# Attention and top-2 experts on one core: a last attention unit with an order of its own, a tanh router, and the low weight halves on GpSimd

## The chip, the core and the metric

One core of one Trainium2 chip. The time is the device time of one execution in microseconds (us), the median of the runs. The profile shows one execution; its span runs from the first to the last instruction.

## The reference

x is 32 sequences of 128 tokens of 128 features, and ctx has the same shape. Two layers follow each other, each with a residual:

```python
x = x + attention(layernorm(x), ctx, ctx)          # 16 heads of 8, linear attention, causal
# q' = elu(q) + 1, k' = elu(k) + 1; out_t = q'_t . sum_{s<=t} k'_s v_s^T; divided by cumsum(q')
x = x + experts(layernorm(x))
# conf = sigmoid(x conf_w^T + conf_b); bids = conf * wealth; the best two of 8 experts are taken
# weights = softmax(the two best bids); expert: (silu(x gate^T) * (x up^T)) down^T, inner size 512
```

## The kernel before

One program writes an order of instructions by hand for each engine, and semaphores tie them together. It has two stages.

**Attention stage.** The 32 sequences are taken in eight units (u = 0 to 7) of four sequences b. `body(u)` of each engine works on unit u and, interleaved with it, on the front of unit u+1 (layer norm, projections, elu) and on the tail of unit u-1 (output projection, second layer norm, router, the places of its tokens among the experts). On TensorE the attention itself is `scores(u, b)` (L1206) and `values(u, b)` (L1223). ScalarE copies the off-diagonal scores (`off_scores`, L693), VectorE masks the diagonal ones (`mask_scores`, L894). VectorE scans Z (`front_z`), and Z's inverse is a seed by an Exp on ScalarE (`z_seed`), `front_zerr` (L884), two Squares (`z_series`) and `front_rz` (L889, L892). `tail_o` (L906) multiplies the values by it, and `tail_out` (L1248 the bias, L1252 the projection) goes to x by `tail_x1` (L911). GpSimd makes the inverse deviation of both layer norms (`front`, `tail`, L481 to L486).

The router of unit u-1 is: logits (L1263, L1266), `tail_exp1` (L714) on ScalarE, add, reciprocal, multiply by wealth on VectorE (L926 to L928), the maxima (L931) and their difference (L933), `tail_exp2` (L720) on ScalarE, and `tail_weights` (L499 to L507) on GpSimd, with a power that takes the inverse. `tail_choose` (L945 to L949), `tail_rank` (TensorE) and `tail_place` (L954 to L964) find the row of each token. GpSimd's `tail_rows` (L513) makes the low halves of the rows and `scatter` (L527) writes them by indirect DMA to the DRAM array by_expert, one unit later; eight scatters a unit.

Each expert's weights (gate, up and down, m = 0 to 2) are loaded to `w_raw` (two buffers) and split in two float16 halves: w_hi on ScalarE (`weights`, L634, three instructions) and w_lo on VectorE (L970, three instructions). Expert u is split in unit u. The load of expert u into its buffer waits, on SP's queue, until the low halves of expert u-2 are made; the loads of the next units stand behind it in that queue.

In unit 7 the same `body` runs without the front of a unit 8; it also has `full_count`, `full_segments` and `full_tiles` (L984 to L998), the table of the first 16 tiles. On GpSimd it sends half of unit 5's rows, then makes unit 6's deviation (`tail(6)`), and then sends the rest of unit 5. The tail of unit 7 and the dispatch of units 6 and 7 lie in the first tiles of the next stage.

**Tile stage.** Rows that chose the same expert are taken in 31 tiles of 256 and then 9 of 128. SP loads a tile's rows with a transposing DMA (L432), the first only when all the rows of units 0 to 5 have been dispatched. TensorE does `gate_up` (L1360 to L1362) of tile i, then `down` (L1380 to L1382) of tile i-1. ScalarE does Silu (L785) and the high half (L792), VectorE the product (L1126) and the low half (L1132); GpSimd writes the result rows to by_token (L616). At the end by_token is read back, added to x and stored. Silu is in another table of ScalarE than Exp: `silu_warm` (L815) stands between the stages, and the router of unit 7 comes back to Exp in tile 4.

Lines of the order that the prediction uses, GpSimd in unit 7 and after it:

```python
if last(u): dispatch(u - 2, [0, 1])
if not first(u): tail(u - 1)
...
dispatch(u - 2, [2, 3]); tail_weights(u - 1, 1 - par)
tail_rows(6); dispatch(6, range(3)); tail(7); dispatch(6, [3])
```

## Time and profile before

| | us |
|---|---|
| median of 3 runs | 402.58 |
| the runs | 405.7, 402.58, 398.73 |
| span of the profiled execution | 364.5 |
| median less span | 38.1 |
| units 1 to 6, from one L906 to the next | 20.0 each |
| unit 7, from its L906 of unit 6 (151.38) to the first gate matmul (177.27) | 25.9 |

The profiled execution's own time is not marked among the runs; the table gives its span. The difference to the median is the time before the first and after the last instruction, to within the spread of the runs (7.0 us). The page's busy shares are: TensorE 81%, VectorE 76%, ScalarE 64%, GpSimd 57% of the span.

### The profile page before, as it was taken

What the parts mean: (1) busy time and instruction counts of PE and PEld (TensorE: products, weight loads), DVE (VectorE), ACT (ScalarE), POOL (GpSimd) and SP (SyncE); (2) the same over time, 40 slices, a digit from 0 to 9 for tenths busy, and PEclk for the clock granted to TensorE, in tenths of its full rate; (3) what the DMA queues carried; (4) which work ended last, traced back from release to release, by engine and by line L of the source; (5) the groups of instructions that cost most, each with busy time, mean ns of one, the idle gap of its engine ahead of it and who ended that gap; (6) DMA issues with size and microseconds to landing.
All of it is one profiled execution on the core that took longest, in us unless ns stands there. A gap on an engine that the chain in (4) does not pass through costs nothing.

```text
span 364.5 us, 12299 instructions
## 1 busy us (share of the span) xinstructions
PE 297.0 (81%) x4430; PEld 246.5 (68%) x4430; DVE 276.2 (76%) x770; ACT 232.9 (64%) x464; POOL 207.5 (57%) x301
## 2 busy tenths in 40 slices
PE   7678897979798888777998899999999799998200
PEld 5456675747475656566687789999988689987100
DVE  5898999999999999993675687976666466564165
ACT  3686969777795959613649786777676476665100
POOL 6301137787868787884686758777554245463300
PEclk9999999999999999755599999999999899999755
DMA  7413120505051310110333314547675796321098
GB/s 239 154 23 125 46 104 10 187 12 190 17 174 34 110 54 21 42 32 31 59 76 74 58 43 104 152 86 170 153 218 154 143 213 161 69 70 28 18 349 325
DMA packets 47722, 39.45 MB, mean 108 GB/s; under 512 B 32550, under 2 KB 39084, under 8 KB 47664
## 3 DMA queue, kind: packets, MB, share of 16 engines
q1 hardware_dynamic: 43344, 30.20, 30.6%
q0 software_dynamic: 4320, 8.47, 8.0%
q8 instruction: 38, 0.62, 0.7%
q14 instruction: 20, 0.16, 0.2%
HBM read 15.16 MB, written 12.21 MB: 75 GB/s over the span
## 4 chain that ended last, share of the span: by engine, by line
PE 29%; DVE 27%; SPq 10%; POOL 10%; issue 9%; DMA 7%; ACT 7%; POOLq 0%; DVEq 0%; ACTq 0%
DVE Pm L899 6%; POOL by_expert L527 5%; SPq L432 3%; PE bank L1360 3%; DMA w_hi<-by_token 3%; PE bank L1380 2%; DVE w_lo L970 2%; PE bank L1362 2%; PE bank L1361 2%; PE scores L1362 2%; PE scores L1361 2%; PE scores L1360 2%; PE bank L1381 2%; PE bank L1382 2%; DVE stats L823 2%
## 5 line engine op out<-in xcount | busy, mean ns | idle before, releaser
L616 POOL DMA_INDIRECT by_token<-y_sb,row_meta x71 | 72.3, 1018 | 61.1 <-ACT y_sb L776 45.3
L1126 DVE SCALAR_TENSOR_TENSOR hid<-scores,silu 128x512 f32<-128x512 f32 x71 | 48.4, 690 | 44.3 <-PE scores L1362 38.6
L527 POOL DMA_INDIRECT by_expert<-token_rows,rows_to x64 | 63.9, 999 | 23.1 <-issue 17.1
L785 ACT ACTIVATE silu<-bank 128x512 f32<-128x512 f32 x71 | 42.0, 596 | 30.0 <-PE bank L1362 29.6
L792 ACT ACTIVATE hid_hi<-hid 128x512 f16<-128x512 f32 x71 | 44.2, 628 | 20.1 <-DVE hid L1126 19.0
L1219 PE MATMUL scores<-qT,Kexp 32*128 32x128 f32 (+1 forms) x1024 | 40.1, 294 | 20.5 <-DVE Pm L899 17.5
L1132 DVE TENSOR_TENSOR Kexp<-hid,hid_hi 128x512 f16<-128x512 f32 x71 | 48.3, 690 | 10.3 <-ACT hid_hi L792 7.5
L1219 PEld LDWEIGHTS scores<-qT,Kexp 32*128 32x128 f32 x1024 | 35.2, 203 | 29.3 <-DVE Pm L899 24.5
L1380 PE MATMUL bank<-w_hi,hid_hi 128*128 x248 | 43.7, 220 | 0.2 <-DVE Kexp L1132 0.2
L1381 PE MATMUL bank<-w_lo,hid_hi 128*128 x248 | 43.6, 220 | 0.0
L1382 PE MATMUL bank<-w_hi,Kexp 128*128 x248 | 43.5, 220 | 0.0
L899 DVE TENSOR_TENSOR Pm<-scores,causal 128x512 f32<-128x512 f32 x64 | 41.1, 684 | 2.3 <-ACT Pm L698 1.8
L1360 PE MATMUL bank<-xgT,w_hi 128*128 128x256 f16 x124 | 34.7, 280 | 6.4 <-DMA xgT<-by_expert 3.6
L698 ACT ACTIVATE Pm<-scores 128x512 f32<-128x512 f32 x32 | 18.8, 586 | 30.5 <-PE scores L1219 30.5
L1361 PE MATMUL bank<-xgT,w_hi 128*128 128x256 f16 x124 | 34.7, 280 | 0.0
L1362 PE MATMUL bank<-xgT,w_lo 128*128 128x256 f16 x124 | 34.7, 280 | 0.0
L1360 PE MATMUL scores<-xgT,w_hi 128*128 128x256 f16 x124 | 34.5, 278 | 0.0
L1361 PE MATMUL scores<-xgT,w_hi 128*128 128x256 f16 x124 | 34.4, 278 | 0.0
L1362 PE MATMUL scores<-xgT,w_lo 128*128 128x256 f16 x124 | 34.4, 278 | 0.0
L1235 PE MATMUL bank<-Pm,Vexp 128*32 128x64 f32 (+1 forms) x1024 | 30.3, 264 | 1.6 <-DVE Pm L899 1.6
L1235 PEld LDWEIGHTS bank<-Pm,Vexp 128*32 128x32 f32 x1024 | 24.5, 117 | 7.4 <-issue 3.3
L1380 PEld LDWEIGHTS bank<-w_hi,hid_hi 128*128 128x128 f16 x248 | 24.5, 99 | 0.7 <-issue 0.4
(291 smaller groups left out, 729.7 us busy)
## 6 DMA issues: line engine op xcount, KB each, us to landing
w_raw<-in_w_pack_dram SPq DMA_DIRECT2D x8, 768.0 KB
x_all<-in_x_tok_dram SPq DMA_DIRECT2D x8, 256.0 KB, 5.6
cT<-in_ctx_t_dram SPq DMA_DIRECT2D x8, 256.0 KB, 5.4
w_hi<-by_token SPq DMA_DIRECT2D x4, 512.0 KB, 7.5
w_lo<-by_token SPq DMA_DIRECT2D x4, 512.0 KB, 8.1
out_dram<-x_all SPq DMA_DIRECT2D x8, 256.0 KB, 6.1
by_expert<-pad_row SPq DMA_DIRECT2D x9, 130.0 KB
by_token<-y_sb,row_meta POOLq DMA_INDIRECT x71
```

The costliest lines, as they stand in the source:

```text
L527: pool.indirect_dma_start(by_expert, bass.IndirectOffsetOnAxis(ap=rows_to[u % 2][:, s, b:b + 1], axis=0), token_rows[u % 2][:, b, s, :], N ...
L616: pool.indirect_dma_start(by_token, bass.IndirectOffsetOnAxis(ap=row_number[:, i % METAS, s, 1:2], axis=0), y_sb[:, k, s, :], None, bounds ...
L899: dve.tensor_tensor(Pm[:, b % 2, :, at:at + CH].rearrange("p (r j) t -> p r j t", r=RG), score_groups[:, :, :, at:at + CH], causal[:].unsq ...
L1126: dve.scalar_tensor_tensor(hid[:, slot, :], bank[2 + slot], 1.0 / WSCALE, silu[:, slot, :], ALU.mult, ALU.mult).then_inc(hid_done, 1)
L1219: ins = pe.matmul(scores4[:, r, j * SPAN + at:j * SPAN + at + n], Kexp[par][rows, c, 2 * j:2 * j + 2, :], qT[par][rows, c * CH:c * CH + n] ...
L1235: ins = pe.matmul(bank[6][32 * r:32 * r + 32, c * CH:c * CH + n], Vexp[par][:, c, 2 * r:2 * r + 2, :].rearrange("p g k -> p (g k)")[:, 16 ...
L1360: pe.matmul(ps, high, x_hi, start=(c == 0), stop=False, skip_group_check=True)
L1361: pe.matmul(ps, high, x_lo, start=False, stop=False, skip_group_check=True)
L1362: ins = pe.matmul(ps, low, x_hi, start=False, stop=True, skip_group_check=True)
L1380: pe.matmul(ps, hid_hi[:, k % 2, slot, h], high, start=(c == 0 and s == 0), stop=False, skip_group_check=True)
L1381: pe.matmul(ps, hid_hi[:, k % 2, slot, h], low, start=False, stop=False, skip_group_check=True)
L1382: ins = pe.matmul(ps, hid_lo[:, k % 2, slot, h], high, start=False, stop=(c == IC - 1), skip_group_check=True)
```

## The change

- Unit 7 gets a `last_body` of its own on TensorE, ScalarE, VectorE and GpSimd. `tail_out(7)` moves from tile 0 to the end of the unit; `tail_rank(6)` and `tail_place(6)` move from the unit to tile 0. The warm-up of Silu moves into the unit, behind the last Exp.
- The router computes sigmoid and the softmax of two by Tanh. VectorE's three instructions L926 to L928 become one. GpSimd's four (L499 to L507) become two small ScalarE instructions that write the weights.
- The high halves of an expert are made one unit ahead (expert 0 before unit 0, expert 1 at the end of unit 0, expert u+1 in unit u from then on). The low halves of experts 0 to 2 are made on GpSimd, with two instructions for each of three parts (a multiplication in place and a subtraction), in units 0 and 1; those of experts 3 to 7 on VectorE in units 2 to 6. SP's waits for a free buffer follow.

```diff
 # GpSimd
+            def low(x, m):
+                pool.wait_ge(whi_done, 3 * x + m + 1)
+                cols = slice(x * (3 * I) + m * I, x * (3 * I) + (m + 1) * I)
+                pool.tensor_scalar(w_raw[x % 2][:, m, :], w_raw[x % 2][:, m, :], WSCALE, None, ALU.mult).then_inc(wx_done, 1)
+                pool.wait_ge(wx_done, 3 * x + m + 1)
+                pool.tensor_tensor(w_lo[:, cols], w_raw[x % 2][:, m, :], w_hi[:, cols], ALU.subtract).then_inc(wlo_pool, 1)
             def body(u, par):
+                front(u + 1)
+                if first(u):
+                    for m in range(3):
+                        low(0, m)
+                    for m in range(2):
+                        low(1, m)
+                if u == 1:
+                    low(1, 2)
                 if u >= 2:
                     tail_rows(u - 2, par)
                 if not first(u):
                     tail(u - 1)
+                if u == 1:
+                    for m in range(3):
+                        low(2, m)
...
+            def last_body(u, par):
+                tail_rows(u - 2, par)
+                dispatch(u - 2, [0, 1])
+                tail(u - 1)
+                dispatch(u - 2, [2, 3])
+                tail_rows(u - 1, 1 - par)
+                tail(u)
+                dispatch(u - 1, [0, 1])
             def tile_step(i, k):
...
+                if i < 2:
+                    dispatch(UNITS - 2, [2 + i])
-                if i == 4:
-                    tail_weights(UNITS - 1, (UNITS - 1) % 2)
 # ScalarE
-                act.activation(conf_e[:], tail_bank(u)[...], ACT.Exp, scale=-1.0).then_inc(lg_exp, 1)
+                act.activation(conf_t[:], tail_bank(u)[...], ACT.Tanh, scale=0.5).then_inc(lg_tanh, 1)
-                act.activation(vexp[:], vdiff[:], ACT.Exp).then_inc(vexp_act, 1)
+                act.activation(vtanh[:], vdiff[:], ACT.Tanh, scale=0.5).then_inc(vtanh_done, 1)
+            def tail_weights(u, par):
+                act.wait_ge(vtanh_done, u + 1)
+                for s, sign in enumerate((-1.0, 1.0)):
+                    act.activation(token_rows[par][:, :, s, D], vtanh[:], ACT.Identity, bias=half_scale[:],
+                                   scale=sign * 0.5 / WSCALE).then_inc(weights_done, 1)
+            def last_body(u, par):
+                off_scores(u, 0)
+                off_scores(u, 1)
+                z_seed(u)
+                off_scores(u, 2)
+                tail_norm(u - 1, 1 - par)
+                act.activation(silu_warm[:], bq_one[:], ACT.Silu)
+                off_scores(u, 3)
+                tail_x2(u - 1, 1 - par)
+                z_series(u)
+                tail_rows(u - 1, 1 - par)
+                tail_tanh1(u - 1)
+                tail_tanh2(u - 1)
+                tail_weights(u - 1, 1 - par)
 # VectorE
-                done(dve.tensor_scalar(conf[:], conf_e[:], 1.0, None, ALU.add))
-                done(dve.reciprocal(conf_e[:], conf[:]))
-                done(dve.tensor_tensor(bids[:], conf_e[:], wealth_b.unsqueeze(1).to_broadcast([P, UB, E]), ALU.mult))
+                dve.scalar_tensor_tensor(bids[:], conf_t[:], 1.0, wealth_half[:].unsqueeze(1).to_broadcast([P, UB, E]),
+                                         ALU.add, ALU.mult).then_inc(router, 1)
+            def last_body(u, par):
+                tail_o(u - 1, 1 - par)
+                full_segments()
+                mask_scores(u, 0)
+                tail_x1(u - 1)
+                tail_stats(u - 1)
+                tail_aggregate(u - 1)
+                mask_scores(u, 1)
+                front_z(u, par)
+                full_tiles()
+                mask_scores(u, 2)
+                front_zerr(u)
+                mask_scores(u, 3)
+                front_rz(u)
+                tail_o(u, par)
+                tail_bids(u - 1)
+                tail_choose(u - 1)
             def tile_step(i, k):
+                if i == 0:
+                    tail_x1(UNITS - 1)
                 hidden(i, k, 0)
+                if i == 0:
+                    tail_place(UNITS - 2)
 # TensorE
+            def last_body(u, par):
+                full_count()
+                tail_out(u - 1)
+                scores(u, par, 1)
+                values(u, par, 0)
+                scores(u, par, 2)
+                values(u, par, 1)
+                scores(u, par, 3)
+                tail_x2(u - 1, 1 - par)
+                values(u, par, 2)
+                tail_logits(u - 1)
+                values(u, par, 3)
+                tail_out(u)
 # TensorE, tile 0
-                        tail_out(UNITS - 1)
+                        tail_rank(UNITS - 2)
 # SP
-                    sp.wait_ge(wlo_done, 3 * (u - 1))
+                if 2 <= u < 2 + POOL_LOWS:
+                    sp.wait_ge(wlo_pool, 3 * (u - 1))
+                elif u >= 2:
+                    sp.wait_ge(wlo_dve, 3 * (u - 1 - POOL_LOWS))
```

## Rows read from the trace of the kernel before

**Rows 1.** The page: TensorE's granted clock in 40 slices of the span.
```profile
PEclk9999999999999999755599999999999899999755
```

**Rows 2.** Busy us of each engine in stretches (stretch, length, engines, clock, DMA share, GB/s).
```profile
111.00:131.00 20.00, 17.00 (x333) 12.61 (x332) 19.42 (x72) 15.69 (x31) 16.23 (x25) 1.00 0.27 75
131.00:151.00 20.00, 14.94 (x293) 10.89 (x291) 19.41 (x72) 15.69 (x31) 16.21 (x25) 0.99 0.09 30
151.00:161.00 10.00, 8.62 (x99) 6.33 (x95) 9.30 (x31) 2.75 (x5) 8.05 (x11) 0.50 0.09 28
161.00:171.00 10.00, 6.55 (x78) 5.73 (x78) 5.01 (x11) 3.45 (x7) 7.26 (x9) 0.50 0.13 42
192.00:202.00 10.00, 8.38 (x87) 7.19 (x85) 5.72 (x9) 8.45 (x18) 6.98 (x8) 1.00 0.31 74
202.00:212.00 10.00, 8.27 (x99) 7.38 (x97) 6.99 (x29) 8.43 (x16) 5.46 (x6) 1.00 0.27 48
212.00:232.00 20.00, 19.97 (x247) 18.52 (x245) 16.61 (x39) 14.65 (x30) 15.69 (x18) 1.00 0.42 102
```

**Rows 3.** Timeline of unit 6: the router on VectorE (start us, us, instruction).
```profile
145.56 0.17 DVE L926 TENSOR_SCALAR conf<-conf_e 128x32 f32<-128x32 f32 x1
...
146.39 0.16 DVE L931 MAX8 top<-bids 128x8 f32<-128x8 f32 x1
```

**Rows 4.** Timeline of unit 0, and GpSimd's wait before unit 1.
```profile
15.93 1.66 ACT L634 ACTIVATE w_hi<-w_raw 128x512 f16<-128x512 f32 x3
...
23.36 1.87 DVE L970 SCALAR_TENSOR_TENSOR w_lo<-w_raw,w_hi 128x512 f16<-128x512 f32 x3
23.41 0.60 ACT L698 ACTIVATE Pm<-scores 128x512 f32<-128x512 f32 x1 [0.86 <-PE scores L1219]
...
33.30 0.20 POOL L481 TENSOR_TENSOR nm<-zero,mv 128x4 f32<-128x4 f32 x1 [19.79 <-DVE mv L827]
```

**Rows 5.** Timeline of unit 1: low halves on VectorE beside ScalarE.
```profile
41.15 1.87 DVE L970 SCALAR_TENSOR_TENSOR w_lo<-w_raw,w_hi 128x512 f16<-128x512 f32 x3
...
42.06 0.58 ACT L698 ACTIVATE Pm<-scores 128x512 f32<-128x512 f32 x1
```

**Rows 6.** Timeline of unit 7.
```profile
152.19 2.07 PE L1248 MATMUL bank<-vo_s,ones 1*128 1x512 f32 x2
...
154.03 2.28 POOL L513 TENSOR_TENSOR token_rows<-x2hat,token_rows 128x512 f16<-128x512 f32 x2
154.19 2.08 PE L1252 MATMUL bank<-vo_s,oT 128*128 128x128 f32 x8
154.53 1.93 DVE L993 TENSOR_TENSOR full_passed<-full_no,full_to 1x128 f32<-1x128 f32 x1
156.20 1.99 PE L1219 MATMUL scores<-qT,Kexp 32*128 32x128 f32 x32
...
158.11 1.51 PE L1235 MATMUL bank<-Pm,Vexp 128*32 128x128 f32 x32
...
164.73 1.65 ACT L638 ACTIVATE x2hat<-x_all,shift,rstd 128x128 f32<-128x128 f32 x4 [1.02 <-POOL shift L486]
...
166.43 1.12 PE L1258 MATMUL bank<-ident,x2hat 128*128 128x128 f32 x4 [3.39 <-ACT x2hat L638]
...
169.47 1.88 PE L1266 MATMUL bank<-vo_s,x2T 128*128 128x8 f32 x8
...
171.99 1.31 SPq L432 DMA_TRANSPOSE xgT<-by_expert  x1
...
177.27 0.39 PE L1360 MATMUL bank<-xgT,w_hi 128*128 128x256 f16 x1 [0.26 <-issue]
```

**Rows 7.** Timeline of tiles 1 to 4.
```profile
183.92 0.27 PE L1360 MATMUL bank<-xgT,w_hi 128*128 128x256 f16 x1
...
202.66 1.28 ACT L714 ACT_TABLE_LOAD   x1
```

**Rows 8.** Waits in 184 to 213 us (engine, line, releaser: us, times, longest).
```profile
PE bank L1360 <- DVE hid L1126: 2.3, 2, 1.5
...
PE scores L1258 <- ACT x2hat L638: 0.8, 1, 0.8
```

205 lines of the change are left out of this document (82 added, 123 removed).

## The prediction

> **What bounds the kernel now.** First the busy times by stretch. In a steady unit VectorE works 19.4 of 20 us and TensorE 17.0; ScalarE and GpSimd have some 4 us left [rows 2]. So a unit is as long as VectorE's list, and an edit there counts if no other engine is late by then. Second the clock. The page shows full clock up to 146 us and then four slices near half [rows 1]; in the stretches it is 1.00 in units 1 to 5, 0.99 in unit 6, 0.50 in unit 7 [rows 2]: the level of 1.2 GHz in place of 2.4 GHz. Ahead of the fall TensorE had only 14.9 us of work in 20, since unit 6 has no values of a later unit to project. Third the timeline of unit 7: from VectorE's oT at 151.4 to the first gate matmul at 177.3 are 25.9 us where other units take 20. Fourth the tiles: TensorE works 8.38 and 8.27 of 10 us from 192 to 212, and 19.97 of 20 behind them [rows 2]. There is idle time to win in the first tiles and none in the middle ones.
>
> **Unit 0.** The high halves of expert 0 stood in ScalarE's way for 1.66 us and the low halves in VectorE's for 1.87 us [rows 4]. Both go: ScalarE makes the first in an idle stretch before 15.4 us, the weights having been asked for at 2.7 us and being there in time, as I take it. I follow the semaphores: without w_hi, off_scores(1) comes 0.85 us earlier; without w_lo, the mask of b=2 starts at 23.2 in place of 25.15. Then ScalarE's copy of b=3 (behind the Kexp copies) is late next, and oT starts 1.25 us earlier, not 3.5. I take 1.0, and bound it by 0 and 2.0. Expert 1's high halves (1.66) stand at the end of unit 0, where ScalarE waits for the next scores.
>
> **Low halves, units 1 to 7.** In unit 1 w_lo ends at 43.0, but ScalarE's copy of b=2, which the next mask waits for, ends at 42.64 [rows 5]. VectorE's 1.87 us lie beside that wait, so taking them away is worth at most 0.4; I take 0. In units 2 to 6 they stay, one expert later, at the same place. Unit 7 has none, and gains nothing there: TensorE decides.
>
> **Low halves on GpSimd.** It was idle for 19.8 us in unit 0 [rows 4]. A subtraction is the form of L513, 2.28 for two, 1.14 each [rows 6]. For the multiplication there is no row; between a tenth of a us (memsets) and 1.14 I take 0.9, near L513. Nine pairs are 18 us. Expert 0's run from 14 to 20 us. Expert 1's first two parts wait for ScalarE at 29.3 and end at 33.8; GpSimd's front(2) would start at 32.0, so its result comes 1.8 us later, at 35.5, where ScalarE wants it at 35.2: 0.3 us lost. Expert 2's run from 39 to 46 and block nobody; SP asks for experts 2 to 4 earlier than now. Cost 0.3, from 0 to 2.
>
> **Tanh router, units 1 to 6.** L926 starts at 145.56 and the first maximum at 146.39, 0.83 us [rows 3]. One instruction of the same size, 0.2 us, and its start-up leave 0.24: 0.59 saved in each unit. The mask of b=3 behind it waits for ScalarE at 147.12, the Squares end at 148.4, and the values of b=3 then follow the mask; none is late. Six units: 3.5 us, from 2.5 to 3.9. GpSimd loses about 2.3 us of weights a unit, hidden but useful in unit 7. ScalarE gains two instructions of 0.2 to 0.3 us beside its 4 us of slack. The start of unit 7, T0, moves from 151.4 to 151.4 - 1.0 + 0.3 - 3.5 = 147.2.
>
> **Unit 7.** TensorE's list at half clock, from rows of this unit [rows 6]: bias 2.07, projection 2.08, three scores of 1.99, four values of 1.51, transposes 1.12, logits 0.63 + 1.88, then again 2.07 and 2.08 for tail_out(7), and 0.2 for the count: 24.1 us. Before, it waited 3.4 us for x2hat, which GpSimd's sends delayed to 164.7; now the transposes stand behind all scores, when x2hat (T0+12.8) is there. Walking it with the masks, it starts at T0+0.7, loses 1.0 more, and reaches tile 0 at T0+25.8, with tail_out(7) done. Tile 0's 24 matmuls at 0.213 are 5.1, tail_rank 0.5: tile 1 starts at T0+31.4. Before it started at 183.92 [rows 7], T0+32.5. Gain at half clock: 1.1 us only, since it is TensorE's work that fills the unit.
>
> At full clock the same walk ends at T0+20.2, and then a load is late: the first transposing DMA waits for unit 5's rows. GpSimd's tail_rows is at T0+1.1, four sends of 1.26, tail 2.0, four sends, landing: SP starts at T0+18.6 (before 171.99, T0+20.6 [rows 6]). The rows took at most 5.3 us more; I take 4.8: T0+23.4. Then 2.6 + 0.3: tile 1 at T0+26.3, gain 6.2.
>
> Which clock? In unit 6 the router's 0.59 us brings TensorE's last values and scores closer: between 147.0 and 150.4 it worked 1.3 us before the fall; the same stretch would now hold 1.9. So I expect the clock to outlast unit 6. In unit 7 VectorE's masks leave it idle for 1.75 and 2.45 us in the first 11 us, and it falls there, near T0+10. The rest at half clock reaches tile 0 at T0+24, and tile 1 at T0+29.6: gain 2.9. This is the value I take; 1.1 and 6.2 are the ends.
>
> The two small additions are free: full_tiles has lost its 1.93 us instruction, which ran while GpSimd's L513 did [rows 6], and stands beside TensorE's work.
>
> **Tiles 0 to 8.** TensorE waited 2.3 us for hid and 0.8 for x2hat [rows 8]. The first hid was late because ScalarE stood in x2hat, for which GpSimd had first sent six of unit 6's rows; now tail(7) stands before those sends. The second was late by the table loads of 1.28 us at 202.66 and again before tile 5's Silu [rows 7]. If Tanh is in Silu's table both go. I take 2.8, from 1.0 (Tanh elsewhere) to 3.4 (all idle of 192 to 212 [rows 2]). Behind 212 the tiles follow TensorE, and the DMAs of the late tiles are bound to tile numbers: the shift stays.
>
> **Sum.** 1.0 - 0.3 + 3.5 + 2.9 + 2.8 = 9.9 us: a span of 354.6 for 364.5, and 402.6 - 9.9 = 392.7 us for the median. Which of the listed runs was profiled is not known; they differ by 7 us, about what a clock that falls at another moment costs, so the sum inherits that doubt.
>
> **Rivals.**
> - *Clock falls as before (25%).* For: units of the old length fell there. Gain 1.1 in place of 2.9: 394.5.
> - *Clock holds through unit 7 (10%).* For: five units kept it with waits of 1 to 1.5 us. Against: waits of 2.4 us now. Gain 6.2: 389.4.
> - *GpSimd and VectorE take turns (8%).* L993 took 1.93 us beside L513, against some 0.28 for its siblings. If every VectorE instruction with two SBUF inputs in units 0 and 1 (four scans, Z times the seed, two of rz, each unit) waits so for low halves, up to 0.5 us each, 7 us go: 399.7. Against: scans have 1.8 us of cover. The Trainium skill (SBUF — State Buffer, "SBUF: two separate sides") calls it an exclusive lock held for a whole instruction, taken by whichever starts first; L993 agrees, and by it a pair of low halves could hold a scan twice.
> - *Tanh shares no table with Exp (4%): the slower side.* Two loads of 1.28 a unit, before tanh1 and before the next front_exp. The first delays the bids, on VectorE's list, by 1.28; the second ScalarE's copy of b=1, now 0.1 us ahead of its mask, by 1.2. Six units: 14.9 us, 407.6. It decides from 0.85 a load. The Trainium skill (ScalarE: Activation LUTs, "Table sets: the hidden batching unit") puts tanh in exp's set; no row here shows it, and by it the case is void. That section does not say where Silu is.
> - *The change does little (4%).* VectorE's gain is eaten by a wait for ScalarE in each unit and unit 7 stays: 401.
>
> **Chances.** Forecast 49%. A measurement can tell about 2%, so faster means below 394.5. The forecast's case lies there 9 times in 10, the second half the time, the third always: 0.44 + 0.12 + 0.10, lowered for the runs' spread to 0.63. Slower by over 2%: 0.03, from the table case at its worst. The rest, 0.34, is within 2%. Range 387 to 399: the third case with a good run at one end, the turns of GpSimd at the other.
>
> **What would show it.** Right: L906 19.4 us apart in units 2 to 6 (unit 1 may differ); the scalar_tensor_tensor of the bids as one instruction; no table load at tile 4 and only one in unit 7; the first gate matmul near 171, with L1252 of unit 7 before it; TensorE busy over 9 of 10 us in tiles 2 to 5. Wrong: granted clock 0.50 from the same place and TensorE full, then 394.5; ACT_TABLE_LOAD within units, then the slow case; L879, L884, L889 longer than 0.7 us in units 0 and 1, then the turns; SP's L432 of tile 0 the releaser of the first gate matmul, then GpSimd's sends bound unit 7.

## The result, and the profile after

| | kernel before | changed kernel |
|---|---|---|
| median of the runs, us | 403.02 (398.73 to 405.7, 4 runs) | 414.16 (410.32 to 416.02, 4 runs) |
| span of the profiled execution, us | 364.5 | 408.5 |

The ratio is 1.0283, interval 1.0212 to 1.0354: slower. Forecast were 392.7 us and a range of 387 to 399. The prediction was wrong in sign. Ratios here and below leave out executions more than 1.5% above the fastest of their kernel, while the medians are of all, so a ratio can differ a little from the quotient of two medians.

The two spans can't be set against each other. The profiled execution of the changed kernel took 410.32 us with a span of 408.5, so 1.8 us lie outside a span, and not 38. One fact is needed for everything that follows: the experiments ran on six chips, and the kernel before takes 405 and 406 us on one of them (here chip 9, met in two sessions, with a quick chip between them), and 365 to 367 us on the five others. Which chip the measured comparison had is not on record. Its times are those of a chip like chip 9 (below: the slower chip); the trace of before, from which the prediction was made, is like those of the five (below: the quick chips).

The changed kernel's page, of the measured comparison: span, busy times, slices and TensorE's clock (for rows 1).

```profile
span 408.5 us, 12268 instructions
PE 322.9 (79%) x4430; PEld 261.6 (64%) x4430; DVE 270.3 (66%) x746; ACT 231.7 (57%) x478; POOL 218.0 (53%) x286
DVE  5988797696977889665670485358647557545445
PEclk9999898698998989666896699698999999999955
```

VectorE, which works 19.4 of 20 us in rows 2, is nine tenths busy in only five of the 17 slices up to unit 7, and the clock dips in the units, where rows 1 show none. The same kernel on one of the five chips (run e5 below, span 353.9 us) has this page:

```profile
PE 291.5 (82%) x4430; PEld 243.7 (69%) x4430; DVE 271.4 (77%) x746; ACT 233.2 (66%) x478; POOL 216.7 (61%) x286
PEclk9899999999999999985799999999999899999855
```

The busy times of VectorE, ScalarE and GpSimd agree within 1.5 us. The engines do the same work and stand more. Stretches of the changed kernel first on the slower chip and then on the quick one (units 2 to 6, unit 7 to the first gate matmul, to the Silu of tile 4, to that of tile 12; columns as in rows 2):

```profile
52.40:171.00 118.60, 97.03 (x1565) 72.07 (x1565) 95.88 (x347) 80.24 (x165) 68.17 (x99) 0.89 0.18 57
171.00:199.00 28.00, 22.71 (x291) 17.81 (x292) 16.71 (x56) 9.69 (x19) 15.45 (x20) 0.68 0.16 38
199.00:230.00 31.00, 22.99 (x196) 18.06 (x196) 13.59 (x37) 13.80 (x28) 14.88 (x18) 0.78 0.23 48
230.00:277.00 47.00, 38.60 (x401) 32.92 (x400) 26.93 (x71) 23.19 (x52) 28.33 (x28) 0.90 0.33 81
```

```profile
54.90:151.80 96.90, 81.59 (x1594) 61.10 (x1594) 94.29 (x347) 80.38 (x165) 68.58 (x100) 1.00 0.22 70
151.80:174.20 22.40, 18.41 (x260) 14.88 (x261) 17.46 (x54) 9.40 (x18) 15.38 (x20) 0.67 0.13 38
174.20:193.70 19.50, 18.76 (x196) 16.21 (x195) 13.93 (x41) 13.86 (x30) 9.28 (x12) 0.95 0.41 69
193.70:226.40 32.70, 32.59 (x398) 30.22 (x397) 28.02 (x71) 23.85 (x53) 26.57 (x26) 1.00 0.45 98
```

In the 196 matmuls up to tile 4 TensorE idles 8.0 us of 31.0 on the slower chip and 0.7 of 19.5 on the quick one. What it stands for is in the waits. Here are two rows of the measured comparison's execution (releaser: us, times, longest). "issue" is time in which the profile shows nothing to wait for. "remote" is a wait that a semaphore ended at a moment near which the profile has the end of no instruction that raises it.

```profile
PE bank L1421 <- issue: 5.9, 7, 1.2
ACT conf_t L719 <- remote: 12.1, 5, 2.5
```

In the whole quick execution TensorE's matmuls have 1.1 us at issue, in the slower one 29.0, and the quick one has no remote wait at all.

The place in unit 4 where this happens first, on the slower chip: ScalarE, TensorE, VectorE, GpSimd in four answers of the timeline.

```profile
113.91 0.72 ACT L689 ACTIVATE zinv<-Z,seed_bias 128x512 f32<-128x512 int32 x1
117.05 0.20 ACT L719 ACTIVATE conf_t<-bank 128x32 f32<-128x32 f32 x1 [2.42 <-remote]
```

```profile
113.88 1.06 PE L1297 MATMUL bank<-vo_s,x2T 128*128 128x8 f32 x8
114.87 1.06 PE L1250 MATMUL scores<-qT,Kexp 32*128 32x128 f32 x16
116.21 0.52 PE L1250 MATMUL scores<-qT,Kexp 32*128 32x128 f32 x6 [0.29 <-issue]
116.96 0.65 PE L1250 MATMUL scores<-qT,Kexp 32*128 32x128 f32 x10 [0.23 <-issue]
```

```profile
117.28 0.19 DVE L943 SCALAR_TENSOR_TENSOR bids<-conf_t,wealth_half 128x32 f32<-128x32 f32 x1 [1.78 <-ACT conf_t L719]
```

```profile
114.19 0.96 POOL L515 DMA_INDIRECT by_expert<-token_rows,rows_to  x1 [0.31 <-issue]
115.45 0.96 POOL L515 DMA_INDIRECT by_expert<-token_rows,rows_to  x1 [0.30 <-issue]
117.52 0.96 POOL L515 DMA_INDIRECT by_expert<-token_rows,rows_to  x1 [1.11 <-ACT conf_t L719]
```

TensorE's scores, one group of 32 without a break on a quick chip, come in three pieces. The logits ahead of them end at 114.94, but matmuls' ends are modelled. The semaphore that the last of them raises goes up at 117.03 in the trace, 2.09 us later, and ScalarE, idle since 114.6, starts 0.02 us behind it; VectorE then waits 1.78 us for ScalarE. So it isn't ScalarE that stops with its inputs ready. TensorE's signal is late: it stops for about two microseconds, of which its own rows show 0.52 us as idle. That holds for all 26 remote waits of ScalarE in this execution (68.2 us): each ends 0.02 us behind a semaphore that TensorE raises. VectorE has six more (21.4 us). On the quick chip, in unit 3, the same semaphore goes up at 88.08, within 0.02 us of the modelled end of the matmul, and ScalarE waits 0.35 us:

```profile
88.10 0.20 ACT L719 ACTIVATE conf_t<-bank 128x32 f32<-128x32 f32 x1 [0.35 <-PE bank L1297]
```

The kernel before has this stop on the slower chip too. The next one, in the changed kernel only, is shown with e8.

### The profile page after: what moved, and what is told of

Its sections match the earlier page's. It is cut to its first block, busy times and chain, and to the rows that moved or that the text cites. A ratio compares the mean times of both kernels' runs of the same rounds, so it can differ in the third digit from the quotient of the medians.

```text
span 408.5 us, 12268 instructions
## 1 busy us (share of the span) xinstructions
PE 322.9 (79%) x4430; PEld 261.6 (64%) x4430; DVE 270.3 (66%) x746; ACT 231.7 (57%) x478; POOL 218.0 (53%) x286
## 4 chain that ended last, share of the span: by engine, by line
PE 51%; DVE 17%; issue 11%; ACT 9%; another core or an unknown queue 6%; DMA 3%; SPq 1%; POOLq 0%; DVEq 0%; ACTq 0%
PE scores L1250 5%; PE bank L1266 4%; PE bank L1400 4%; PE bank L1402 4%; PE bank L1420 4%; PE bank L1421 4%; PE bank L1422 3%; PE bank L1401 3%; PE scores L1400 3%; PE scores L1402 3%; PE bank L1234 3%; PE scores L1401 3%; DVE Pm L925 3%; DVE Vexp L897 2%
## 5 line engine op out<-in xcount | busy, mean ns | idle before, releaser
L619 POOL DMA_INDIRECT by_token<-y_sb,row_meta x71 | 76.5, 1077 | 77.7 <-ACT y_sb L802 64.4
L515 POOL DMA_INDIRECT by_expert<-token_rows,rows_to x64 | 64.4, 1006 | 47.5 <-PE bank L1266 20.4
L1250 PE MATMUL scores<-qT,Kexp 32*128 32x128 f32 (+1 forms) x1024 | 45.4, 301 | 21.2 <-DVE Pm L925 17.6
L1250 PEld LDWEIGHTS scores<-qT,Kexp 32*128 32x128 f32 x1024 | 38.8, 206 | 32.0 <-DVE Pm L925 24.7
L811 ACT ACTIVATE silu<-bank 128x512 f32<-128x512 f32 x71 | 40.5, 597 | 31.8 <-remote 24.1
L818 ACT ACTIVATE hid_hi<-hid 128x512 f16<-128x512 f32 x71 | 44.1, 629 | 23.5 <-DVE hid L1155 11.9
L1421 PE MATMUL bank<-w_lo,hid_hi 128*128 x248 | 45.3, 224 | 5.9 <-issue 5.9
L1420 PE MATMUL bank<-w_hi,hid_hi 128*128 x248 | 45.4, 224 | 5.1 <-issue 4.7
L1422 PE MATMUL bank<-w_hi,Kexp 128*128 x248 | 45.5, 224 | 3.6 <-issue 3.3
L1266 PE MATMUL bank<-Pm,Vexp 128*32 128x64 f32 (+1 forms) x1024 | 38.5, 281 | 6.9 <-issue 5.8
L1266 PEld LDWEIGHTS bank<-Pm,Vexp 128*32 128x32 f32 x1024 | 29.3, 124 | 16.5 <-issue 13.1
L802 ACT ACTIVATE y_sb<-bank,row_meta 128x128 f32<-128x128 f32 x71 | 22.3, 358 | 26.3 <-remote 20.5
```

The source lines that it names most:

```text
L515: pool.indirect_dma_start(by_expert, bass.IndirectOffsetOnAxis(ap=rows_to[u % 2][:, s, b:b + 1], axis=0), token_rows[u % 2][:, b, s, :], N ...
L619: pool.indirect_dma_start(by_token, bass.IndirectOffsetOnAxis(ap=row_number[:, i % METAS, s, 1:2], axis=0), y_sb[:, k, s, :], None, bounds ...
L1250: ins = pe.matmul(scores4[:, r, j * SPAN + at:j * SPAN + at + n], Kexp[par][rows, c, 2 * j:2 * j + 2, :], qT[par][rows, c * CH:c * CH + n] ...
L1266: ins = pe.matmul(bank[6][32 * r:32 * r + 32, c * CH:c * CH + n], Vexp[par][:, c, 2 * r:2 * r + 2, :].rearrange("p g k -> p (g k)")[:, 16 ...
L1420: pe.matmul(ps, hid_hi[:, k % 2, slot, h], high, start=(c == 0 and s == 0), stop=False, skip_group_check=True)
L1421: pe.matmul(ps, hid_hi[:, k % 2, slot, h], low, start=False, stop=False, skip_group_check=True)
```

## The experiments

Kernels that ran together share a chip and its runs of the kernel before. Chip 14 had e1 to e4, chip 8 e5 to e7, **chip 9 e8 to e10**, chip 2 e11 to e14, **chip 9 again e15 and e16**, chip 10 e17, chip 15 e18. So the theories formed on the way were about "conditions"; that these are chips shows only in the list of all.

**e1, the kernel before once more**, as a reference for pauses and spans. Edit: none.

> The kernel before, unchanged. Its profiled execution had a span of 364.5 us, its timed ones took 399 to 406; the changed kernel's span is 408.5 us for a time of 410.3, so only 1.8 us lie outside a span. Theory A (the first profile was a rare execution): a new profile has a span of about 397 to 403 us, units of 22 to 24 us in place of 20.0, and the pauses of TensorE inside a stream of matmuls with nothing waited for (label issue; 2.9 us before, 29.1 after) are 20 us or more. Theory B (the pauses come with the change): the span is near 365 again, the pauses near 3 us, units of 20.0.

367.05 us beside 365.85, ratio 1.0043 (1.0 to 1.0087), span 366.3, and 3.0 us of TensorE's idle time put to issue. The stretches are those of the trace of before (20.0 us a unit). So that trace is no rarity, but it isn't that of the runs at 403.

**e2, the tanh router alone.** Edit, as short as it goes:

```diff
-                    tail_exp2(u - 1)
+                    tail_tanh2(u - 1)
+                    tail_weights(u - 1, 1 - par)      # on ScalarE
...
                     scatter(u - 2, 2, 1)
-                    tail_weights(u - 1, 1 - par)      # on GpSimd
+                    pool.wait_ge(off_done, UB * u + 4)
                     scatter(u - 2, 3, 0)
```

> The kernel before with the tanh router alone: one VectorE instruction for three, weights on ScalarE, none on GpSimd; weights split and last unit as before. If the router is what costs (its two ScalarE instructions, or the missing power on GpSimd that paced the scatters), this is slower than before by most of the 11 us. If the cost lies in the last unit or in the low halves, this is 1 to 5 us faster than before (0.59 us a unit on VectorE, two table loads fewer).

357.48 us, 0.9758 (0.9671 to 0.9846). The units are 19.4 us long but one, of 21.8 us, where the clock dips. No table load is left at tiles 4 and 5. The gain, 8.4 us by the medians, is more than the 3.5 + 2.8 forecast for router and tiles.

**e3, router and low halves** (e2 with `low(x, m)` on GpSimd for experts 0 to 2, `weights(u + 1)` on VectorE).

> The tanh router and the new places of the weight halves (experts 0 to 2 on GpSimd), the last unit as before. If GpSimd's 18 instructions in units 0 and 1 or the earlier weight loads cost, this is over 5 us slower than the run with the router alone; if they are neutral, within 2 us of it. If the last unit's order is to blame for the 11 us, this stays at or below the time of before.

357.18 us, 0.976 (0.9658 to 0.9862): no better than e2. Unit 1 takes 22.7 us for e2's 19.4.

**e4 and e7, router and last unit's order** (the changed kernel with the low halves back in their own unit).

> The tanh router and the last unit's own order, the weight halves where they were before. If the last unit's order costs (tail_out(7) in front of tile 0, a clock that falls in it), this is about as slow as the changed kernel, 412 to 416 us, and the run without it is not. If it gains as forecast, this is 3 us below the run with the router alone.

> The tanh router and the last unit's order again, since its first four times lay 9 us apart (353.0 to 361.7). If the spread comes from where TensorE's clock falls and returns, the times lie again between 351 and 362 with a mean 2 to 4 us below the router alone; if the order of the last unit brings nothing, they lie at 356 to 358.

0.9692 (0.9556 to 0.9828) and 0.969 (0.96 to 0.9781). From unit 7's oT to the first gate matmul: e2 24.8 us, e7 24.3; to the Silu of tile 4 another 21.8 and 19.0. So in e7's profiled execution this part pays 3 us, in the tiles. In e4's, where the clock is at half through all of unit 7, it pays nothing: 27.1 and 20.1. By the medians both (357.85 and 356.32 us) are level with the router alone on two chips (357.48, 356.16 in e13). One of e7's six executions took 501.28 us, for which the record has no reason.

**e5, the changed kernel again.**

> The changed kernel, unchanged. Its profiled execution has 29.1 us of TensorE pauses with nothing waited for and spent 408.5 us; the kernel before, run again, had 3.0 us of them, a span of 366.3 and a time of 366 to 367 in place of 403. Theory A (the pauses belong to the conditions of the first measurement, not to the change): the pauses are near 3 us, and the time is 353 to 359 against 366 of the kernel before, that is 2 to 4% faster, near the forecast gain of 9.9 us. Theory B (the change makes the pauses): 29 us of pauses again, a time over 370.

354.97 us beside 364.92: 0.9729 (0.9683 to 0.9775), **faster** by 9.95 us. The same kernel is 2.7% faster on this chip and 2.8% slower in the measured comparison.

**e6, the low halves alone** on the kernel before.

> The kernel before with the weight halves moved (experts 0 to 2 on GpSimd, the others a unit ahead) and nothing else. Run with the router it changed nothing (357.2 against 357.5). My prediction gave it 1.0 less 0.3 us. If it is neutral: within 1.5 us of before. If ScalarE or GpSimd in units 0 and 1 eat the gain: unit 0 ends near 32 us and unit 1 takes over 20.

366.43 us, 1.0044 (1.0008 to 1.008): unit 1 takes 23.4 us. The reason, from e5, where GpSimd works on w_lo in unit 1:

```profile
45.34 1.50 POOL L529 TENSOR_SCALAR w_raw<-w_raw 128x512 f32<-128x512 f32 x1
46.92 1.16 POOL L531 TENSOR_TENSOR w_lo<-w_raw,w_hi 128x512 f16<-128x512 f32 x1
48.04 1.93 POOL L529 TENSOR_SCALAR w_raw<-w_raw 128x512 f32<-128x512 f32 x1
```

```profile
46.96 1.67 DVE L910 TENSOR_TENSOR Z<-Z,zinv 128x512 f32<-128x512 f32 x1
48.55 0.59 DVE L943 SCALAR_TENSOR_TENSOR bids<-conf_t,wealth_half 128x32 f32<-128x32 f32 x1
50.34 1.02 DVE L964 TENSOR_TENSOR hot<-iota,topi 128x32 f32<-128x32 f32 x2
```

and the same three instructions of VectorE in e10, where GpSimd has none of it in this unit:

```profile
44.36 0.68 DVE L900 TENSOR_TENSOR Z<-Z,zinv 128x512 f32<-128x512 f32 x1
44.95 0.19 DVE L933 SCALAR_TENSOR_TENSOR bids<-conf_t,wealth_half 128x32 f32<-128x32 f32 x1
46.34 0.29 DVE L954 TENSOR_TENSOR hot<-iota,topi 128x32 f32<-128x32 f32 x2
```

VectorE's instructions with two inputs in SBUF grow by 1.0, 0.4 and 0.7 us. The first and the third meet a subtraction (L531; the one at 50.06 is not shown) and grow by about what is left of it. The second meets a multiplication (L529) and grows by 0.4 us, with 1.4 us of it left, while the multiplication takes 1.93 us for its usual 1.49. The Trainium skill (SBUF — State Buffer, "SBUF: two separate sides") describes a lock between the two engines for a whole instruction. The rows beside the subtractions agree; the one beside the multiplication shows a shorter wait.

These three make 2.1 of the 3.3 us. The other 1.2 are there before the first of them: L910 starts 14.75 us behind unit 0's oT in e5 and 13.60 in e10, though e10 has the low halves (1.87 us) on VectorE ahead of it. In e5 GpSimd's pairs for expert 1 end at 36.4, ahead of its part of the layer norm (front(2)), and ScalarE waits 0.68 and 0.61 us for GpSimd's two shifts.

**e8 and e9, before and changed kernel with more loads.** Theory then: the changed kernel's early loads of experts' weights delay the fetching of instructions. Both kernels load every expert's weights twice more, into a buffer that nobody reads yet, so the extra loads are no part of the computation.

```diff
+                if u >= 1:
+                    sp.wait_ge(extra, 32 * u)
+                for j in range(2):
+                    sp.dma_start(single_more[:, j, :].bitcast(F32), w_pack[bass.ds(u, 1), :, :].rearrange("o p i -> p (o i)")).then_inc(extra, 16)
```

> The kernel before, and behind each expert's load two more loads of the same 768 KB into a tile that nobody reads in this stage; the output is unchanged. The slow execution's pauses of TensorE begin, in each unit, some 2 us after SP has issued an expert's load. Theory C (instructions arrive by DMA and stand behind such loads): 4 us more of transfers in each unit bring pauses here too, 1 to 4 us a unit, 10 to 30 us in all, and the time rises to 375 to 395. Theory D (the pauses have another cause, in the place where the first measurement ran): no new pauses, a time within 3 us of 365.

> The changed kernel with the same two extra loads behind each expert's load. Theory C: pauses of 10 to 30 us as in the kernel before with them; and if the first measurement's 11 us against the change came from pauses, the change loses its 10 us here or more (a ratio near 1). Theory D: 355 within 3 us, and the change keeps its 10 us.

Both ran on chip 9: before 405.13 (17 executions, 397.93 to 409.77); e8 413.71, 1.0226 (1.0104 to 1.0347); e9 420.89, 1.0426 (1.0336 to 1.0515). The forecasts had been written for a chip that takes 365 us, so their times can't be read here. The added loads cost both kernels alike, most of it in unit 0 (37.5 and 37.3 us; the changed kernel without them 29.7), and units 2 to 6 of the changed kernel are as long with them (118.4 us) as without (118.6). So more loads bring no more pauses, and the theory falls in this form. What stays is a pair, e9 and e8, of changed kernel and before on the same chip, profiled both. The changed kernel's units have a second stop, of which e8 shows none. First unit 4 of the changed kernel on the slower chip, TensorE and GpSimd (its values of b=2 are one group of 32, 0.87 us long, when nothing interrupts):

```profile
118.56 0.75 PE L1266 MATMUL bank<-Pm,Vexp 128*32 128x128 f32 x23
119.55 0.26 PE L1266 MATMUL bank<-Pm,Vexp 128*32 128x64 f32 x2 [0.23 <-issue]
120.30 0.26 PE L1266 MATMUL bank<-Pm,Vexp 128*32 128x64 f32 x2 [0.50 <-issue]
```

```profile
118.78 0.95 POOL L515 DMA_INDIRECT by_expert<-token_rows,rows_to  x1 [0.30 <-issue]
120.04 0.96 POOL L515 DMA_INDIRECT by_expert<-token_rows,rows_to  x1 [0.30 <-issue]
```

Then unit 5 of e8, where the router's weights stand between the sends:

```profile
144.50 0.96 POOL L533 DMA_INDIRECT by_expert<-token_rows,rows_to  x1 [1.27 <-ACT conf_e L720]
145.77 0.96 POOL L533 DMA_INDIRECT by_expert<-token_rows,rows_to  x1 [0.30 <-issue]
...
147.66 1.05 POOL L507 TENSOR_TENSOR wts<-vsum,minus_one 128x4 f32<-128x4 f32 x1
...
149.93 1.03 POOL L533 DMA_INDIRECT by_expert<-token_rows,rows_to  x1 [0.15 <-issue]
```

```profile
146.60 1.25 PE L1241 MATMUL bank<-Pm,Vexp 128*32 128x128 f32 x32
```

This is one unbroken group; the changed kernel's breaks twice more, by 0.47 and 0.51 us, before it ends at 122.1. In the changed kernel three sends follow each other 1.26 us apart (the first of them is the 117.52 above), in e8 two. On the quick chip such rows do no harm: in unit 3 of e5 seven sends follow each other from 85.84 to 93.46, and TensorE has one pause of 0.23 us beside them.

**e10, one expert on GpSimd** (changed kernel, expert 0's low halves on GpSimd, the others' on VectorE in their own unit; `POOL_LOWS = 1`).

> The changed kernel with only expert 0's low halves on GpSimd (unit 0); expert u's high and low halves lie in unit u again for u = 1 to 7. In the changed kernel unit 1 takes 22.7 us, since GpSimd's products and subtractions meet VectorE's instructions with two SBUF inputs (Z times the seed 1.67 for 0.68, hot 1.02 for 0.34). If that is the cause, unit 1 takes 19.4 here and the time falls by 1 to 3 us below the changed kernel, 352 to 354; unit 7 may give 1 us back for its weights. If the cause is the high halves' place, unit 1 stays over 21 us.

407.08 us, 1.01 (1.0036 to 1.0164) on chip 9; the measured comparison gave 1.0283. Unit 1 is 19.4 us. The high halves are back in their own unit here too, so this run alone doesn't tell the low halves from them; the rows shown with e6 do. Unit 7 up to the first gate matmul is longer in turn, 31.0 us for 28.2.

**The stages side by side.** Start times of oT (L932 in the changed kernel), of the first gate matmul and of the Silus bound them; us.

| stage | before, rows 1 to 8 | e5 changed | e8 before | e9 changed | e16 router only | changed, measured comparison |
|---|---|---|---|---|---|---|
| chip | quick | 8 | 9, more loads | 9, more loads | 9 | slower |
| unit 0 | 31.3 | 32.2 | 37.5 | 37.3 | 31.1 | 29.7 |
| unit 1 | 20.0 | 22.7 | 20.0 | 22.7 | 19.4 | 22.7 |
| units 2 to 6 | 100.1 | 96.9 | 115.6 | 118.4 | 118.8 | 118.6 |
| unit 7 to first gate | 25.9 | 22.4 | 28.7 | 28.5 | 29.0 | 28.2 |
| to Silu of tile 4 | 23.5 | 19.6 | 25.7 | 31.2 | 24.4 | 31.0 |
| in it, TensorE's tile 3 | 5.4 | 5.3 | 5.6 | 16.7 | 5.6 | 16.4 |
| to Silu of tile 12 | 34.5 | 32.6 | 47.4 | 47.6 | 45.9 | 47.0 |
| to the end | 129.3 | 127.6 | 136.5 | 134.7 | 134.6 | 131.4 |
| TensorE at issue, units 2 to 6 | 0.9 | 0.2 | 2.8 | 7.8 | 8.4 | 7.3 |
| at issue, first gate to tile 4 | 0.3 | 0 | 2.4 | 7.4 | 2.6 | 7.1 |
| ScalarE at remote, units 2 to 6 | 0 | 0 | 14.3 | 12.0 | 12.2 | 12.1 |
| at remote, first gate to tile 4 | 0 | 0 | 5.0 | 11.8 | 5.7 | 11.0 |

(The last four lines sum the rows of the waits of each stretch with this releaser; those of TensorE count matmuls alone. Tile 3 goes from its first matmul to that of tile 4.) Between before and e5 the changed kernel wins 10.6 us on the quick chips; between e8 and e9 it loses 9.1. The difference of 19.6 lies in units 2 to 6 (6.0), the first tiles (9.4), unit 7 (3.2) and tiles 4 to 12 (2.2; the other stages give 1.2 back). In the first two the matmuls' idle time at issue grows by 5.0 and 5.1 us from e8 to e9. The loss in the first tiles is a single tile, tile 3, 11 us longer in e9 than in e8.

How far one can lean on this: before was profiled on chip 9 once, with more loads, and its executions there lie 12 us apart. Units 2 to 6 take 118.2 to 119.1 us in all five traces of tanh kernels on the slower chips and 115.6 in this one of before. e16's profiled execution took 405.06 us, 2.2 more than its median. The step in tile 3 is far above such a spread.

**e11 and e15, the new run of sends taken apart.** Theory E: the router's weights kept sends apart on GpSimd, and without them a third send in a row stops TensorE.

```diff
-                    pool.wait_ge(off_done, UB * u + 4)
+                    pool.wait_ge(av_done, UB * u + 4)
                     scatter(u - 2, 3, 0)
-                    pool.wait_ge(av_done, UB * u + 4)
                     scatter(u - 2, 3, 1)
```

> The changed kernel with one edit: the send of (slot 0, batch 3) waits for the unit's last values, as the send of (slot 1, batch 3) does, so the third, fourth and fifth GpSimd sends in a row of each unit (at +16.4, +17.7 and +18.9 us behind oT in the changed kernel's trace) become two at +16.4 and +17.7 and two behind the unit's end. Theory E (in the slower condition TensorE's stream pauses right behind the third of a run of sends spaced 1.26 us, and taking tail_weights off GpSimd made a second such run in every unit): where the kernel before reads 403, the pauses at +18 to +20 go, units 3 to 6 take 22 to 23 us in place of 23.1 to 24.8, and the time falls by 4 to 8 us below the changed kernel's 414, to a ratio of 1.01 to 1.02. Rival F (the pauses have to do with the place in TensorE's own stream, its instruction fetches, not with the sends): pauses stay at +18 to +20, ratio 1.025 to 1.035. Where the kernel before reads 365, both expect no change from the changed kernel's 355 (0.5 us at most from sends in front of the next unit's front shift), ratio 0.97 to 0.977.

> The kernel of e11 again, for the slower condition, since e11 fell in the quick one, where it measured 0.980 (the changed kernel 0.973). Theory E: where the kernel before reads 403, TensorE's pauses at +18 to +20 of the units are gone and the ratio is 1.01 to 1.02. Rival F (the place in TensorE's own stream): pauses stay, 1.025 to 1.035. In the quick condition 0.975 to 0.985 again.

e11 (chip 2): 0.9802 (0.9755 to 0.9849). e15 (chip 9): 414.48 us beside 406.43, 1.0232 (1.0012 to 1.0453). The interval holds both theories. The profile says more: TensorE's idle time at issue in units 2 to 6 falls from 7.3 to 3.5 us, as E wants, but the units take 118.2 us for 118.6. TensorE's late signals haven't become fewer: ScalarE's waits that end with one grow in units 2 to 6 from 12.1 to 25.6 us, seven for five. One row of them in e15:

```profile
ACT Pm L702 <- remote: 20.8, 5, 5.6
```

The sends before now start later (12.5 us behind oT for 11.6, since the pair stands ahead of GpSimd's next front), and stand in a row of their own: in unit 3 of e15 five of them from 12.5 to 17.9. TensorE's pauses at issue there end at 16.1, 18.3 and 19.7 us behind oT, those of the changed kernel's unit 3 at 15.2, 15.9, 18.4, 19.2 and 20.6. E had units 3 to 6 at 22 to 23 us each; they take 22.5 to 24.7. So the gain of 4 to 8 us isn't in the stages, though the times alone (1.0012 to 1.0453) don't exclude it. That pauses move with the sends is seen. That three sends in a row are needed is not: at the start of unit 3 TensorE's signal is 2.08 us late behind the moved pair alone (78.17 and 79.44).

**e12, the kernel before with its router weights behind the send.**

```diff
-                    tail_weights(u - 1, 1 - par)
                     scatter(u - 2, 3, 0)
+                    tail_weights(u - 1, 1 - par)
```

> The kernel before with one edit the other way: GpSimd's router weights (2.5 us, they stood between the sends of (1,2) and (0,3)) stand behind the send of (0,3), so that the second run of three sends arises in the kernel before too. Theory E: in the slower condition units 3 to 6 get pauses at +18 to +20 and 1 to 1.5 us more each, ratio 1.012 to 1.02; in the quick condition 1.0 (0.997 to 1.005). Rival F: no change in either condition, 0.997 to 1.005.

0.9989 (0.9952 to 1.0027) on chip 2: no difference on a quick chip. It was not run on chip 9, so it says nothing about E there.

**e13 and e16, the router alone, on two more chips.**

> The tanh router alone on the kernel before, as e2. Theory E: it is this edit that joins the sends, so in the slower condition it carries most of the loss: its gain of 8.9 us is eaten by 8 to 14 us of pauses in units 3 to 7 and the first tiles, ratio 0.995 to 1.02 and pauses at +18 to +20. Rival G (the slower condition punishes the last unit's new order or the low halves' early loads, not the router): ratio 0.975 to 0.985. In the quick condition both expect 0.976 again.

> The kernel of e13 again, for the slower condition. Theory E: the tanh router carries most of the loss there, 0.995 to 1.02 with pauses at +18 to +20. Rival G (the last unit's order or the low halves carry it): 0.975 to 0.985. In the quick condition 0.976 again.

e13 (chip 2): 356.16 us, 0.9765 (0.9678 to 0.9853), as e2. e16 (chip 9): 402.89 us beside 406.43, 0.9955 (0.9891 to 1.0019). The router's 8.6 us of the quick chips are 3.5 here by the medians, 1.8 by the ratio, and the interval includes none. In units 2 to 6 it has the changed kernel's length (118.8) and idle time at issue (8.4), in the first tiles those of the kernel before (24.4; 2.6). So the longer units come with the router edit, and rival G (0.975 to 0.985), that this edit is innocent, falls. E's 0.995 to 1.02 for this kernel was met.

**e14, e10 with the pair of sends last.**

> The changed kernel with only expert 0's low halves on GpSimd (as e10) and the pair of sends behind the unit's end (as e11): a candidate to beat both. Theory E, slower condition: e10's 1.01 less 4 to 8 us, 0.99 to 1.0; rival F: 1.01 as e10. Quick condition: the changed kernel's 355 less the 3.3 us that unit 1 lost to GpSimd's and VectorE's turns, 351 to 353, ratio 0.963 to 0.968.

0.9742 (0.964 to 0.9845) on chip 2: the expected 0.963 to 0.968 lies at the edge of the interval, and the profile shows what ate the gain. Unit 1 is back at 19.4 us, but unit 7 up to the first gate matmul takes 27.6 us, where the changed kernel and e11, with no weights to split in that unit, take 22.4 and 23.2. VectorE splits expert 7's weights for 1.87 us ahead of a mask, and TensorE waits for this mask; first e14, then e5:

```profile
163.80 1.99 PE L1240 MATMUL scores<-qT,Kexp 32*128 32x128 f32 x32 [2.49 <-DVE Pm L914]
```

```profile
164.95 1.99 PE L1250 MATMUL scores<-qT,Kexp 32*128 32x128 f32 x32 [0.67 <-DVE Pm L925]
```

In e14 the clock stays at half from T0+3.6 to T0+30.9 (T0 is the start of unit 6's oT, where unit 7 begins), in e5 from T0+4.1 to T0+17.7 and for 3.5 us once more. e17 and e18, with the same weights in the unit, have 27.1 us and the clock of e14.

**e17 and e18, unit 6's last sends spread.** In the changed kernel twelve of GpSimd's sends stand in a row at the first tiles (209.6 to 225.1 us of its trace, beside the long tile 3, from 212.2 to 228.6), since `tail(7)` now stands ahead of unit 6's rows. This version, on e10's, uses the idle time ahead of `tail(7)` and then sends one at a time.

```diff
                 tail_rows(u - 1, 1 - par)
+                dispatch(u - 1, [0])
                 tail(u)
-                dispatch(u - 1, [0, 1])
...
-                if i < 2:
-                    dispatch(UNITS - 2, [2 + i])
+                if i < 6:
+                    scatter(UNITS - 2, 1 + i // 2, i % 2)
```

> The kernel of e10 (changed kernel, only expert 0's low halves on GpSimd) with unit 6's last rows sent otherwise: batch 0 ahead of tail(7), where GpSimd stood idle, and the other six one at a time behind the results of tiles 0 to 5, in place of eight between and ahead of those of tiles 0 and 1. Theory E' (in the slower condition TensorE's stream pauses while GpSimd's sends follow each other without a gap; the last unit's order joined unit 6's sends and the first results to 12 in a row): from the first gate matmul to tile 4's Silu 24 to 27 us in place of e10's 30.6 (before with more loads: 25.7), and the ratio 0.99 to 1.003 in place of 1.010 where the kernel before reads 403. Rival H (the first tiles pause for another reason, the order of TensorE's stream itself): 30 to 31 us, 1.005 to 1.015. Where it reads 365: no change from e14's 20.1 us and 0.974, within 0.968 to 0.98, with the unit 1 of 19.4.

> The kernel of e17 again, which fell in the quick condition (0.970 there, the best of all). Theory E' in the slower condition: 24 to 27 us from the first gate matmul to tile 4's Silu in place of 30.6, ratio 0.99 to 1.003. Rival H: 30 to 31 us, 1.005 to 1.015. In the quick condition 0.965 to 0.975.

354.96 us, 0.9699 (0.9609 to 0.9789), and 355.55 us, 0.9725 (0.9676 to 0.9774), on chips 10 and 15. From the first gate matmul to tile 4's Silu they take 20.4 and 20.3 us, as e14 does (20.1). Neither was chip 9, so whether the row of twelve is what stops TensorE in the first tiles stays open.

## Why the prediction was wrong

**The base.** The step that failed is the one of the sum: "a span of 354.6 for 364.5, and 402.6 - 9.9 = 392.7 us for the median". It took the 38.1 us between span and median for a constant outside the span. 1.8 us lie there. The rest was time inside the timed executions that the profiled one did not have: on a slower chip TensorE stops (29.0 us at issue in the changed kernel's execution, and waits of 68.2 us for ScalarE that end with a late signal), and the clock falls with it. There the change costs 2.8% instead of gaining. The prediction knew the gap and put the doubt down to a run's spread of 7 us. No rival covered what was in it, though a gap four times the forecast gain was the largest number on the page that nothing explained.

**On the quick chips the sum held,** partly by luck: 9.9 us forecast, 9.95 measured in e5, by errors against each other. The forecast counted unit 7 up to the first matmul of tile 1, and so does this table.

| term | forecast | quick chips | |
|---|---|---|---|
| unit 0 | 1.0 | 0 or 1.6 | 32.2 for 32.1 (e5, e1) where the clock dips in it; 31.3 to 29.7 (measured comparison) where it doesn't |
| low halves on GpSimd, and unit 1 | -0.3 | -3.3 | 22.7 for 19.4; the turns were a rival at 8% |
| router, six units | 3.5 | 3.6 | 19.4 for 20.0 |
| unit 7 and tile 0 | 2.9 | 6.3 | 26.2 for 32.5 |
| tiles 1 to 12 | 2.8 | 2.9 | 48.4 for 51.3 |
| behind them | 0 | 1.7 | 127.6 for 129.3 |

With -0.9 for unit 0 (32.2 for the 31.3 of the trace of before) the terms make 10.3 of the 10.6 us between the two spans.

- *Router:* right. The bids are one instruction (L943 of unit 4, 0.19 us beside ScalarE's conf_t above), and the saving is the 0.59 of rows 3.
- *Low halves on GpSimd:* mis-sized, beyond the stated 0 to 2. The multiplication takes 1.49 us, not 0.9, the subtraction 1.16 for 1.14. So the pairs end later than forecast and GpSimd's shifts come later: 1.2 us for the forecast's 0.3. The other 2.1 are the rival's mechanism: VectorE's instructions wait for GpSimd's. The forecast priced the turns too low in chance: L993 in rows 6 was one case of just this, and nine pairs of the same kind were being added.
- *Unit 7:* mis-sized, by luck in the good direction; 6.3 is about what the forecast had for a clock that holds (6.2), but the clock did fall, at T0+4.1 and not near T0+10. In e5 (T0 is 151.8) the projection at T0+1.2 still runs at full clock, 1.16 us against the 2.08 of rows 6, and the scores at T0+5.1 at half:

```profile
152.96 1.16 PE L1283 MATMUL bank<-vo_s,oT 128*128 128x128 f32 x8
156.84 1.98 PE L1250 MATMUL scores<-qT,Kexp 32*128 32x128 f32 x32 [2.72 <-DVE Pm L925]
...
174.17 0.42 PE L1400 MATMUL bank<-xgT,w_hi 128*128 128x256 f16 x1
...
176.54 0.27 PE L1400 MATMUL bank<-xgT,w_hi 128*128 128x256 f16 x1
```

  The wait of 2.72 us for the mask lies between them; the forecast had 1.75. The turns made it longer. One small instruction of full_segments, 0.22 us in the trace of before, runs into GpSimd's tail_rows ahead of the mask:

```profile
152.55 2.33 DVE L1003 TENSOR_SCALAR full_u<-full_u 1x8 uint32<-1x8 uint32 x1
152.57 2.28 POOL L501 TENSOR_TENSOR token_rows<-x2hat,token_rows 128x512 f16<-128x512 f32 x2
```

  The prediction called the small additions free because L993 had stood beside L513; the meeting only moved to another instruction. The clock was back at full at T0+17.7 for 3.4 us and for good 2.4 us into tile 0, where the prediction kept it at half from T0+10 to the end of tile 0. And "Unit 7 has none, and gains nothing there: TensorE decides" was wrong: kernels that split weights in this unit reach tile 1 at T0+27.6 to 32.0 (e4, e7, e14, e17, e18), those that don't at T0+26.2 and 26.5 (e5, e11). So on the quick chips, and with the last unit's new order, the low halves' move gives back in unit 7 about what it costs in unit 1.
- *Tiles:* right. Both table loads of rows 7 are gone, so Tanh and Silu need no change of table between them; the table rival (4%) fell with it, since no load stands within the units either. TensorE's waits in tiles 1 to 12 are 0.7 us for 3.3. All of the gain is there when tile 6 starts (22.8 us behind tile 1 for 26.0), at 209.9 in the trace of before, and none comes behind it, as "Behind 212 the tiles follow TensorE" had it.

**On a chip like chip 9** three terms change sign or go: units 2 to 6 lose 2.8 us instead of winning 3.2, through the router edit (e16: 118.8 us alone); the first tiles lose 5.5 instead of winning 3.9, through the last unit's order (31.0, 30.6, 31.4 and 31.2 us in the four kernels with it there, 25.7 and 24.4 in the two without); unit 7 up to the first gate matmul wins 0.3 instead of 3.5. The low halves lose 3.3 in unit 1 on both kinds. In the prediction's terms: it followed each stall along the semaphores, and had no term for a stop in TensorE's own stream, since in the profiled execution there was almost none. "GpSimd loses about 2.3 us of weights a unit, hidden but useful in unit 7" saw only the use of the freed time; in units 2 to 6 the hole is filled with sends.

**Shown, and not shown.** Shown: the kernel before takes 40 us more on chip 9 than on five others, and the change, or a kernel one small edit from it, is faster on the quick chips (e4, e5, e7, e11, e14, e17, e18: 0.969 to 0.980) and slower on chip 9 (e10 and e15: 1.01 and 1.0232; e9 against e8: 7.2 us). The changed kernel itself ran in the measured comparison and on chip 8 alone. Shown too: that the loss of the first tiles lies in tile 3 and comes with the last unit's order. That the units' loss comes with the router edit rests on one trace of before on chip 9. In these two stages TensorE's matmuls stand 10 us more in all for nothing that the profile shows. Not shown: what stops it. The pauses stand behind rows of GpSimd's sends and moved with them in e15, but no time was won there, and the version that spreads the longest row did not meet chip 9. Rival F, a cause in the order of TensorE's own stream or in the fetching of its instructions, is not excluded; against the fetching speaks that the two queues for instructions moved no packet from 112.1 to 119.2 us, around the first stop in unit 4. Why chip 9 has the stops and the others not, with DMA packets no longer in the mean there (38 ns on SP's queue both in the changed kernel's execution of the measured comparison and in e5, 106 and 111 ns for GpSimd's), stays open too.

**A better version.** Of the kernels that ran on chip 9 the router alone is the one that lost nowhere: 0.976 on chips 14 and 2, 0.9955 (interval up to 1.0019) on chip 9. On the quick chips e17 and e18 are as good as any (0.970 and 0.9725), untested on chip 9, where their nearest relative, e10, lost 1.0%. Untried is a version that keeps weights out of unit 7 without nine pairs on GpSimd.

## What to carry to other kernels

Set the profiled execution's span beside the runs before anything is priced from it: a gap much larger than the forecast gain means that the trace isn't of the executions that are timed, and the gap, not the change, is then the first thing to explain. Work put on GpSimd beside VectorE's instructions is not hidden even where both have idle time: a meeting cost VectorE 0.4 to 2.1 us here, and it matters most just ahead of something that TensorE waits for. Taking such a meeting off one instruction can move it to the next. And taking a small computation from between DMA issues is no free gain; where a kernel is measured on several chips, an edit that wins on one should be tried on another before it is kept.

## What the runs showed of the hardware

- One kernel, unchanged, takes 365 to 367 us on five chips and 405 and 406 us on a sixth, 11% more, the same in two sessions. The other engines' instructions have the same durations there (median of Silu 0.60 us, of a mask 0.68, of a send 0.96, in the changed kernel's execution of the measured comparison and in e5). TensorE pauses for 0.2 to 1.2 us (one of 1.7 in e9) with nothing that the profile shows to wait for, and in the units its semaphore goes up 2.0 to 2.1 us behind the modelled end of the matmul, once a unit, while ScalarE waits. The mean granted clock of units 2 to 6 is 0.89 there and 1.00 in e5.
- Every remote wait in the six traces of a slower chip ended with a semaphore that TensorE raises; ScalarE started 0.02 us behind it.
- GpSimd's `tensor_scalar` on 128x512 f32 in SBUF takes 1.49 us, where a `tensor_tensor` of the same size takes 1.16 us.
- A VectorE instruction of 0.68 us took 1.67 us beside GpSimd's subtraction. One of 0.19 us took 0.59 beside its multiplication. One of 0.22 us on a 1x8 tile, with a single input, took 2.33 beside two of GpSimd's subtractions.
